# A two-attention perceiver kernel: the second attention's maxima shared out anew between ScalarE and VectorE, the keys' low weight rows as a pair of half-array products

## What is computed

```
x = x + _L0_xattn_ref(_layernorm(x), ctx_768, ...)   # 16 heads of 16, then a two-layer net
x = x + _L0_attn_ref(_layernorm(x), ...)             # causal self attention
x = x + _L0_ffn_ref(_layernorm(x), ...)              # 8 experts, gelu
x = x + _L1_xattn_ref(_layernorm(x), ctx_768, ...)   # 16 heads of 64: softmax(q k^T) v, then Wo
x = x + _L1_attn_ref(_layernorm(x), ...)
x = x + _L1_ffn_ref(_layernorm(x), ...)              # 8 experts, silu
```

## Time and profile before

| | us |
|---|---|
| median of 3 runs | 1517.76 |
| lowest, highest | 1512.5, 1522.74 |
| the profiled execution | 1513.2 |
| its span, first to last instruction | 1511.5 |
| mean granted TensorE clock | 0.966 of full speed |

### The profile page before, as it was taken

The page is one execution under the profiler, slowest core; times in us unless marked ns, Lnnn a source line. Parts: engine busy times, 40 slices in busy tenths (PEclk is TensorE's granted clock), DMA queues, the critical chain, the costliest instruction groups (busy, mean ns, idle before and its releaser), DMA issues.

```text
span 1511.5 us, 36970 instructions
## 1 busy us (share of the span) xinstructions
PE 1386.6 (92%) x15312; PEld 921.4 (61%) x15312; DVE 1042.2 (69%) x1482; ACT 1062.0 (70%) x1630; POOL 106.4 (7%) x145
## 2 busy tenths in 40 slices
PE   5888887999997598999999979999998999989969
PEld 2444444777775497433333447777776777767758
DVE  6999997000002302999999998888888888887842
ACT  4787776999992133666666658888887888877820
POOL 6232220000000002200000000000000000000000
PEclk9999999999998599999999989999999999999979
DMA  4445437676656054555654567777777677797630
GB/s 138 157 183 185 168 121 200 155 181 148 170 127 223 1 196 136 191 183 201 229 192 179 188 148 147 147 146 146 147 139 146 123 147 143 147 258 136 158 125 4
DMA packets 128794, 236.48 MB, mean 156 GB/s; under 512 B 9244, under 2 KB 114166, under 8 KB 128630
## 3 DMA queue, kind: packets, MB, share of 16 engines
q1 hardware_dynamic: 128630, 234.13, 58.2%
HBM read 155.98 MB, written 78.12 MB: 155 GB/s over the span
## 4 chain that ended last, share of the span: by engine, by line
PE 61%; DVE 21%; issue 11%; ACT 2%; DMA 2%; SPq 2%; POOL 0%; POOLq 0%; DVEq 0%; ACTq 0%
PE ps L692 60%; DVE W L1291 6%; DVE small L1354 5%; DVE p L1291 5%; DMA W<-keys_hi 1%; SPq L405 1%; ACT W L1114 1%; DMA W<-in_ctx_dram 1%; DVE W L1321 1%; DVE q_all L1291 1%; SPq L463 0%; ACT p L1128 0%; DVE ctxT_b L1343 0%; DVE att L1291 0%; DVE ctxT_a_lo L1347 0%
## 5 line engine op out<-in xcount | busy, mean ns | idle before, releaser
L1291 DVE TENSOR_TENSOR p<-ps,p 128x512 f16<-128x512 f32 (+1 forms) x467 | 350.5, 751 | 70.2 <-ACT ps L1091 67.5
L1091 ACT ACTIVATE p<-ps 128x512 f16<-128x512 f32 (+1 forms) x490 | 329.2, 682 | 90.2 <-PE ps L692 88.0
L692 PEld LDWEIGHTS ps<-q_all,W 128*128 128x128 f16 (+1 forms) x3544 | 230.9, 99 | 69.7 <-issue 17.3
L692 PE MATMUL ps<-q_all,W 128*128 128x128 f16 (+2 forms) x3544 | 264.2, 227 | 9.1 <-DMA W<-keys_hi 6.1
L1354 DVE TENSOR_REDUCE small<-ps 128x1 f32<-128x896 f32 x224 | 241.4, 1079 | 4.7 <-PE ps L692 4.3
L1091 ACT ACTIVATE ps<-ps 128x512 f32<-128x512 f32 x392 | 235.8, 602 | 0.0
L692 PE MATMUL ps<-v,p 128*128 128x130 f16 x3136 | 169.7, 206 | 5.4 <-DVE p L1291 3.3
L692 PE MATMUL ps<-wv,ctxT_a_hi 128*128 128x512 f16 (+1 forms) x588 | 155.3, 346 | 10.3 <-DVE W L1321 6.1
L692 PEld LDWEIGHTS ps<-v,p 128*128 128x128 f16 x3136 | 147.4, 97 | 12.2 <-ACT ps L1091 3.6
L692 PE MATMUL ps<-wv,ctxT_b 128*128 128x512 f16 (+1 forms) x588 | 154.5, 344 | 0.0
L1291 DVE TENSOR_TENSOR v<-ps,v 128x512 f16<-128x512 f32 x196 | 135.4, 691 | 15.6 <-ACT v L1186 2.9
(11 more groups left out here) (226 smaller groups left out, 1744.8 us busy)
## 6 DMA issues: line engine op xcount, KB each, us to landing
W<-keys_hi SPq DMA_DIRECT2D x54, 896.0 KB, 14.6
W<-keys_low SPq DMA_DIRECT2D x27, 896.0 KB, 11.7
keys_hi<-p SPq DMA_DIRECT2D x75, 224.0 KB, 2.0
keys_low<-p SPq DMA_DIRECT2D x75, 224.0 KB, 1.9
keys_hi<-W SPq DMA_DIRECT2D x65, 224.0 KB, 2.0
keys_low<-W SPq DMA_DIRECT2D x65, 224.0 KB, 2.0
W<-values SPq DMA_DIRECT2D x14, 960.0 KB, 9.2
W<-in_L_ffn_W_dram SPq DMA_DIRECT2D x10, 1024.0 KB, 8.8
```

The source lines that it names most:

```text
L692: return pe.matmul(out_, lhsT, rhs, start=start, stop=stop, **kw)
L1091: return act.activation(out_, in_, ACT.Exp, scale=scale)
L1291: return dve.tensor_tensor(out_, a, b, op)
```

## The change

1. Maxima of L1. The two heads' scores lie in slots 2 and 3, four banks. ScalarE's copy now takes the first three (128x1344, both banks of the even head and the first of the odd one), VectorE's reduction only the fourth (128x448). `running` and `copied` grow to 1344, and so does the merge. `running` and two of the buffers move within `W`. ScalarE's copy waits for both heads' scores, TensorE's next odd scores for copy and reduction.
2. The end of that pass. One step folds the even head's two banks, three halving steps run over both heads' 448, a last reduction gives 16 numbers, and one more step joins VectorE's own maxima.
3. Keys' low weight rows, in both attentions. The fifth product of each bank had 64 rows of zeros in its weights. Now the low rows stand in both halves of `wk16[:, 3]`, and the two banks' fifth products are of 64 rows, one on each half of the array, issued together behind the eight full ones. For this the second bank's tokens have the high part of `ctxT_b` in rows 64 to 127. The transposes place them so, from the fifth tile of a chunk on. The banks become 512 and 384 tokens (`FIRST = 4` tiles).
4. What follows from 3. The value products need low weights that match either placing: `wv_low`, two variants with zeros in the other half. For L0 the second one is in a free piece of `wv16`, for L1 in `q_max`, which GpSimd blanks and fills once the last scores are made (`low_placed`; TensorE waits for it at the second pass's fifth tile). VectorE makes L1's low key weights twice, GpSimd copies L0's. A blanking of `wk16` falls away, one of `wv16` is added.

```diff
@@ project_keys
-                for n in range(MAXB):
-                    ks = slice(c * CLEN + n * MAXC, c * CLEN + (n + 1) * MAXC)
-                    o = ps[:, 2 * slot + n, 0:MAXC]
+                banks = ((0, FIRST * P), (FIRST * P, CLEN))
+                for n, (k0, k1) in enumerate(banks):
+                    ks = slice(c * CLEN + k0, c * CLEN + k1)
+                    o = ps[:, 2 * slot + n, 0:k1 - k0]
                     mm(o, L.wk16[:, 0, ws], ctxT_a_hi[:, ks], True, False)
                     mm(o, L.wk16[:, 1, ws], ctxT_a_hi[:, ks], False, False)
                     mm(o, L.wk16[:, 0, ws], ctxT_a_lo[:, ks], False, False)
                     mm(o, L.wk16[:, 2, ws], ctxT_b[:, ks], False, False)
-                    ins = mm(o, L.wk16[:, 3, ws], ctxT_b[:, ks], False, True)
+                for n, (k0, k1) in enumerate(banks):
+                    rows = slice(n * CB, (n + 1) * CB)
+                    ins = mm(ps[:, 2 * slot + n, 0:k1 - k0], L.wk16[rows, 3, ws],
+                             ctxT_b[rows, c * CLEN + k0:c * CLEN + k1], False, True)
                 ins.then_inc(keys_summed, 1)
@@ copy_maxima (ScalarE)
-                src = ps[:, 2 * slot:2 * slot + 2, 0:MAXC]
-                act.wait_ge(max_scored, n_max(L, c, h))
+                banks = 2 if L is L0 else 3
+                src = ps[:, 2 * slot:2 * slot + banks, 0:MAXC]
+                act.wait_ge(max_scored, n_max(L, c, h if L is L0 else h + 1))
...
-                act.copy(dst.rearrange("p (n k) -> p n k", n=MAXB), src).then_inc(max_copied, 1)
+                act.copy(dst.rearrange("p (n k) -> p n k", n=banks), src).then_inc(max_copied, 1)
@@ first_pass (VectorE)
+                            ins = dve.tensor_reduce(mpart[:, h // 2, n:n + 1], ps[:, 2 * pair + 1, 0:MAXC], AX.X, ALU.max)
...
+                    last = small[:, 376:384]
+                    dve.tensor_reduce(last, mpart, AX.X, ALU.max)
+                    settle(tt(L.running[:, :, 0:MAXC], L.running[:, :, 0:MAXC], L.running[:, :, MAXC:2 * MAXC], ALU.max))
+                    heads = L.running.rearrange("p u (n k) -> p u n k", n=3)[:, :, 0:3:2, :]
+                    w = MAXC
+                    for _ in range(3):
+                        w //= 2
+                        settle(tt(heads[:, :, :, 0:w], heads[:, :, :, 0:w], heads[:, :, :, w:2 * w], ALU.max))
+                    dve.tensor_reduce(mx_all.rearrange("p (u j) -> p u j", j=2), heads[:, :, :, 0:w], AX.X,
+                                      ALU.max).then_inc(maxima_made, 1)
+                    dve.wait_ge(maxima_made, 2)
+                    settle(tt(reduced, reduced, last.rearrange("p (u k) -> p u k", k=1), ALU.max))
@@ gpsimd, after the second attention's value weights
+            pool.wait_ge(max_scored, n_max(L1, NCH - 1, H - 1))
+            settle(pool.memset(q_max[0:CB, 0:1024].bitcast(F32), 0.0))
+            pool.tensor_copy(q_max[CB:P, 0:1024], wv16[0:CB, 3, :]).then_inc(low_placed, 1)
+            pool.wait_ge(low_placed, 1)
             pool.wait_ge(shift_made, 2)
@@ turn_left
             if is_direct(L, h):
-                return [(max_reduced, N_RED[L.n, n, h])]
+                left = [(max_reduced, N_RED[L.n, n, h])]
+                return left + [(max_copied, N_COP[L.n, n, h - L.apart])] if L is L1 else left
@@ vector, the second attention's key weights
-            dve.scalar_tensor_tensor(out=L1.wk16[0:CB, 3, :], in0=wk_b, scalar=VS, in1=L1.wk16[0:CB, 2, :],
-                                     op0=ALU.mult, op1=ALU.subtract).then_inc(wk_made, 1)
+            for k in range(2):
+                ins = dve.scalar_tensor_tensor(out=L1.wk16[k * CB:(k + 1) * CB, 3, :], in0=wk_b, scalar=VS,
+                                               in1=L1.wk16[0:CB, 2, :], op0=ALU.mult, op1=ALU.subtract)
+            ins.then_inc(wk_made, 1)
```

More of the change, by code:

```diff
@@ L184, in perceiver_kernel @@
         L1.wv, L1.wo = stage[:, 0:2048], stage[:, 2048:4096]
+        L1.wv_low = wv16[:, 3, :], q_max[:, 0:1024]
         L1.wk16 = spare.rearrange("p (a n) -> p a n", a=4)
-        L1.running = W[:, 10752:14336].bitcast(F16).rearrange("p (h k) -> p h k", h=H // 2)
+        L1.running = W[:, 8960:14336].bitcast(F16).rearrange("p (h k) -> p h k", h=H // 2)
         L1.k_parts = ([p16_flat[:, n * CLEN:(n + 1) * CLEN] for n in range(4)]
                       + [W[:, 14784 + 448 * n:14784 + 448 * (n + 1)].bitcast(F16) for n in range(2)])
-        L1.copied = [r.bitcast(F16) for r in (att[:, 0:448], att[:, 448:896], W[:, 14336:14784])]
+        L1.copied = [r.bitcast(F16) for r in (att[:, 0:672], W[:, 7168:7840], W[:, 7840:8512])]
         L1.dram = dram("keys1_hi", (1024, M)), dram("keys1_low", (1024, M))
@@ L205, in perceiver_kernel, with half_of @@
         W1_OFF, W2_OFF, CA_OFF = 7616, 8640, 9664
+        FIRST = 4
+        def half_of(t):
+            return int(t >= FIRST)
         def wview(off, a, b):
@@ L575, in rsqrt_var, with split_weights16 @@
                 pool.tensor_tensor(rstd, rstd, minus_half[:, :], ALU.pow).then_inc(ln_rstd, 1)
-            def split_weights16(w, dst, n):
+            def split_weights16(w, dst, n, low=None):
                 top, rest = w[:, 0:n], w[0:CB, n:2 * n]
@@ L584, in split_weights16 @@
                 settle(pool.tensor_tensor(dst[0:CB, 3, :], rest, dst[0:CB, 2, :], ALU.subtract))
-                return pool.tensor_copy(dst[CB:P, 2, :], rest)
+                ins = pool.tensor_copy(dst[CB:P, 2, :], rest)
+                if low is not None:
+                    ins = pool.tensor_copy(low, dst[0:CB, 3, :])
+                return ins
             pool.memset(ident[:, :], 0.0)
@@ L1313, in keys_low_out @@
                 n = L.k0 + b
-                src = ps[:, 2 * slot:2 * slot + 2, 0:MAXC]
-                hi, low = (k_part(L, b, part).rearrange("p (n k) -> p n k", n=MAXB) for part in range(2))
+                src = ps_row[:, 1024 * slot:1024 * slot + CLEN]
+                hi, low = (k_part(L, b, part) for part in range(2))
                 dve.wait_ge(keys_hi, n + 1)
@@ L1364, in first_pass @@
                 dve.wait_ge(max_reduced, max(v for k, v in N_RED.items() if k[0] == L.n))
[L1365 to L1372 removed]
+                if L is L0:
+                    settle(dve.tensor_reduce(reduced, mpart.rearrange("p (a k) c -> p a k c", k=L.apart), AX.X, ALU.max))
+                    w = CLEN
+                    for _ in range(4):
+                        w //= 2
+                        settle(tt(L.running[:, :, 0:w], L.running[:, :, 0:w], L.running[:, :, w:2 * w], ALU.max))
+                    dve.tensor_reduce(copied, L.running[:, :, 0:w].rearrange("p (a k) w -> p a k w", k=L.apart), AX.X,
+                                      ALU.max).then_inc(maxima_made, 1)
+                    dve.wait_ge(maxima_made, 1)
+                else:
+                    last = small[:, 376:384]
[4 more added lines that the diff above has]
+                    for _ in range(3):
+                        w //= 2
+                        settle(tt(heads[:, :, :, 0:w], heads[:, :, :, 0:w], heads[:, :, :, w:2 * w], ALU.max))
+                    dve.tensor_reduce(mx_all.rearrange("p (u j) -> p u j", j=2), heads[:, :, :, 0:w], AX.X,
+                                      ALU.max).then_inc(maxima_made, 1)
+                    dve.wait_ge(maxima_made, 2)
+                    settle(tt(reduced, reduced, last.rearrange("p (u k) -> p u k", k=1), ALU.max))
                 settle(ts(mx_all, mx_all, -1.0 / VS, EXP_SHIFT, ALU.mult, ALU.add))
```

49 lines of the change are left out of this document (25 added, 24 removed).

## The result

The changed kernel takes 1508.28 us (median of 10 runs, 1505.1 to 1509.07) against 1516.97 for the kernel before on the same chip (median of 10, 1512.5 to 1522.74). The ratio is 0.9943, with a 95% interval of 0.9927 to 0.9958: faster by 0.6%. The forecast was 1500, a gain of 1.15%. So half of the gain is missing, and the experiments look for it.

The account below looks back on a forecast made before the run. VectorE, with TensorE nearly as full, was taken to bound the second attention's first pass. Stage -19.0, end of pass +2.4 and first attention -0.9 gave -17.5 us: 1500 for the median, range 1490 to 1513.

Parts of the forecast that it names:

- What bounds the kernel, and that both engines must be relieved: Second attention's first pass: VectorE full at 2.53 us a block, TensorE at 2.48; relieving VectorE alone is worth 0.05.
- Rival 3: Slower: VectorE's merge leaves the two-per-cycle rate and takes 1.47, deciding from 1.00 on; +49 us, 1568; chance 0.05.
- Rival 1: TensorE's low pair runs in series or is held up by its weight loads; period 2.48, time 1514; chance 0.08.
- The loop through ScalarE: Second attention: keys, keys_out, copy, scores and keys again take 4.71 us for two blocks, 2.355 each, the longest loop.
- 0.09 to S(b+1): In that loop, the hand-over from the end of ScalarE's copy to the next block's scores on TensorE: 0.09 us.
- rival 2: Coupling costs more: near-equal loops, slower three-bank copy or slower hand-over; period 2.40 to 2.48, 1510 at 2.44; chance 0.25.
- The case that I had forecast: Second attention's first pass at a period of 2.30 to 2.39 us a block; chance 0.58.
- my sign of being wrong: The forecast counts as wrong if the time from one block's keys to the next stays above 2.45 us.
- End of the pass: VectorE reduces alone after the second attention's last block: wider folding, a longer last reduction and one more step, +2.4 us.
- The 1.80: End of that pass: VectorE's folding steps cover 3136 more elements, costing about 1.80 us.
- First attention, -0.9: Keys end 0.07 us earlier where they are late once a chunk, in 13 chunks: -0.9 us.
- The costs put at nothing: VectorE's extra low-row step, GpSimd's weight copy and q_max work, SyncE's stores and the transposes: hidden under other work.

Follow-up runs that it names:

- The two halves alone: Two runs on the kernel before: the maxima's new split alone, keys as before (0.9997); the keys' low-row pair alone, maxima as before (0.9992).
- after: The changed kernel with the whole change, against the kernel before: 1508.28 us, ratio 0.9943.

## Why the prediction was right in direction and twice too large

- **What bounds the kernel, and that both engines must be relieved: right.** The two halves alone show it: 0.9997 and 0.9992.
- **VectorE: right.** The reduction's row lasts 0.62 and its start is 0.54 ahead of the next (0.53 forecast). The merge's row lasts 0.86 (0.84 forecast), and its start is 0.83 ahead of the next (0.77 to 0.80 forecast). Rival 3 needed 1.00 or more, so it is out.
- **TensorE: right.** The low pair starts together, and K to K is 2.32 where nothing else holds it, against 2.31 forecast. Rival 1 is out.
- **ScalarE's copy: right.** 1.28 against 1.29.
- **The loop through ScalarE: the right loop, with one term mis-sized.** The step that failed is "0.09 to S(b+1)". It measures 0.26, which is all of the 4.88 - 4.71 = 0.17. Over the stage that is 110 x 0.17 / 2 = 9.3 us: the stage gained 9.7 where I had 19.0. I had read the hand-over from the one place where the scores wait for VectorE through a shorter chain of waits, and had looked in the diff for the work that it moves and not for the wait that it adds, which I put at nothing without a word. This is rival 2's "hand-over each way slower than I read", chance 0.25; it gave 1510 for a period of 2.44, and 2.44 came. The case that I had forecast, a period of 2.30 to 2.39 at 0.58, did not come. The time lies in the range of 1490 to 1513 only because that also covers rival 2, and K to K missed my sign of being wrong, 2.45, by 0.01.
- **End of the pass: nearly right.** +3.0 for +2.4. From the end of the last merge VectorE works alone for 8.2 us (878.14 to 886.30), where 8.4 was forecast and 6.0 it was before. In it the four folding steps take 5.86 (4.24 before, +1.62, forecast 1.80) and the last reduction 0.46 more (0.47). The 1.80 doesn't follow from what stands beside it: 2.44 for 3584 elements gives 2.13 for 3136. What I left out is ahead of the folding. The last merge starts 1.31 behind the last reduction, where it was 1.00, because it waits for the three-bank copy; and it lasts 1.10 instead of 0.61. Of that 0.25 is its greater width. The other 0.24 is missing in the kernel with the maxima only, whose last merge lasts 0.86 and which has no GpSimd work on `q_max`; here GpSimd's copy (876.39 to 877.42) runs into the merge. So an edit that I costed at nothing costs 0.24.
- **First attention, -0.9: can't be seen.** The stage's start scatters over 7 us among the kernels.
- **The account.** On the profiled executions 1495.7 was forecast and 1509.07 measured, 13.4 more: 9.3 in the stage, 0.6 in the tail, 4.0 ahead of the stage (+3.1 for -0.9, within the scatter just named), -0.4 in the rest, all rounded. By the medians of ten runs the gain is 8.7 us for 17.5.
- **The costs put at nothing held** but for that merge and the added wait: with the one wait gone the kernel takes 1497.64, which is 18.4 us less than the 1516.03 measured beside it. So the sum of -17.5 fits a kernel without the added wait. There the stage is 20.8 shorter for 19.0 (2.34 a block for 2.355) and the tail 2.9 longer for 2.4.

## What to carry to other kernels

Where a loop goes from one engine's end to another's start, read the hand-over as a term of its own, and look at which wait stands where: put the wait that ends last on the last instruction, or at least behind the waits that are long past. An added wait for something already waited for isn't free, although only one of the two ever holds anything up. Here it cost 10.6 us, more than half of the 18.4 that the change was worth without it. And when two engines are both nearly full, changes that relieve one of them measure as nothing one by one.

## What the runs showed of the chip

- TensorE takes 0.10 to 0.11 us for each instruction behind the one that a semaphore releases, waits long satisfied among them: 0.06 from the end of ScalarE's copy to the product that waits for it, 0.14 with one behind, 0.20 to 0.26 with two, 0.47 with four. Four more waits ahead of the released instruction cost nothing that can be told (1498.12 against 1497.64).
- The timeline and the waits show it only in part: the gap is put on "ACT" or "issue", and the wait instructions have no rows there. The trace's records of them show it in full: in the run with four behind they start 0.11 apart.
- Two products of 64 rows on the two halves of the array, into different banks, start together, and with other half-array work behind them no second switch is paid: in the first chunk the scores start 0.47 after the last full product (615.77 to 616.24). Of that 0.26 lies between the last full product and the pair (703.63 to 703.89 in the rows of after), which leaves 0.21 for the pair, the length of its 512-column member.
- A ScalarE cast of 128x1344 from three PSUM banks takes 1.28 us, 0.83 ns an element more than the 0.91 of two banks.
- A VectorE maximum of 128x1344 float16 takes 0.86 us alone and 1.10 where GpSimd's copy of 64x1024 float16 runs beside its start (maxima only against after). The merge of 448 elements goes from 0.39 to 0.63 at the same place, so it is a delay of 0.24 and not a slower rate.
- The keys' pair on the array's halves alone shortens a block by 0.17 us in the first chunk, where TensorE paces (2.48 to 2.32), and by 0.002 from the third on, where VectorE does.
